# Later layers' constants, weights and first rows loaded and prepared one stage earlier; the second convolution's first group in quarters

## Chip, core and metric

The kernel runs on one core of a Trainium2 chip. The metric is the time of one execution on the device in microseconds (us), as the median of several runs. The core has five engines: TensorE (PE, matmuls, with its weight loads PEld), VectorE (DVE), ScalarE (ACT), GpSimd (POOL) and SyncE (SP), which issues the DMAs.

## What is computed

Four layers on x of 128 graphs, 64 nodes and 256 features, each x = x + f(relu(layernorm(x))). Layer 0 is two graph convolutions and four LSTM passes, layer 1 an attention over 512 edges. Layers 2 and 3 are what the change is about, together with the tables of layer 1:

```python
# layer 2
A_norm = A + jnp.eye(n, dtype=A.dtype)
deg = jnp.sum(A_norm, axis=0) + jnp.sum(A_norm, axis=1) - jnp.diagonal(A_norm)
dinv = jax.lax.rsqrt(deg)
A_hat = A_norm * dinv[:, None] * dinv[None, :]
agg = jnp.einsum('nm,bmd->bnd', A_hat, features)
h = jax.nn.relu(_batchnorm(agg.reshape(-1, d) @ W1.T + b1, g1, be1))
out = _batchnorm(h @ W2.T + b2, g2, be2)
# layer 3
Wh = jnp.einsum('bnf,fo->bno', h, W)
e = (Wh @ a1)[:, :, None] + (Wh @ a2)[:, None, :]
e = jnp.where(e >= 0, e, ALPHA * e)
e = jnp.where(adj_matrix[None] == 0, -jnp.inf, e)
h_prime = jnp.einsum('bij,bjo->bio', jax.nn.softmax(e, axis=-1), Wh)
```

The batch norms of layer 2 need the mean and variance over all 8192 rows, so each of its two products must be finished over all rows before the next stage can begin.

## The kernel before

The 8192 rows are cut into 16 groups (NG) of 512 rows, a group being four tiles of 128 rows (two graphs each). The program is a row of stages, each a block in which every engine runs its own list of instructions; a stage begins on every engine when all engines have ended the stage before. The order inside an engine is the order of the code, and engines wait for each other by semaphores. fp32 products are made as three passes (lines 49 to 51) over a rounded high half and the low rest of each operand.

- `edge_tables` (line 658) sorts the 512 edges and makes the tables of layer 1. It is one long chain on DVE with short turns to PE. Its last steps on DVE are `t_cut` (774), `s_picked` (776), two small copies, `s_weight` (780), which waits for the matmul `s_pW` (809), and eight `t_src`/`t_dst` comparisons (782, 783). SP issues the stage's loads and then the first rows of the next stage. POOL makes low halves of weights there.
- `edge_attention` (813) is layer 1, in four quarters. It ends with additions to rows `c_x` (1426), each stored to `x2` in HBM by SP (920), and SP waits for the last stores to land (line 943).
- `conv_first` (1470) begins with its loads (1511 to 1515): eight small constants, the first two groups of rows `d_xt`, and W1 and W2. DVE adds the identity to the adjacency, PE sums it to degrees, POOL takes deg to the power -0.5 (line 1534, one column), PE spreads that over the columns (1544), and DVE writes `d_hat` (1669). For each group then: statistics on DVE (1616 to 1625), POOL's power -0.5 over four columns (1531), `d_xn` on DVE (1632), relu `d_h` on ACT (1592), aggregation on PE (1561), high half `d_ghi` on ACT (1602), low half `d_glo` on DVE (1681), W1 on PE, the bias on ACT into `H` (1586) and statistics of `H` on DVE (1638). W1 is split before the loop and W2 after it (1643, 1644).
- `conv_second` (1697) loads three small vectors (1719), DVE finishes the first batch norm (1732 to 1737), and for each group ACT makes `f_r` in four instructions (1770), DVE its high and low half (1742, 1744), PE the product with W2, ACT stores it to `H` (1779), DVE takes statistics (1750).
- `dense_attention` (1812) is layer 3. It loads its constants and the first two groups (1879, 1881), finishes the second batch norm (2079 to 2084), folds the vectors a1, a2 into W (2088, 2090), splits W, makes the mask (2098 to 2105), and runs the 16 groups.

## Time and profile before

| | us |
|---|---|
| median of 3 runs | 2231.93 |
| runs | 2231.73 to 2234.61 |
| the profiled execution, its time | 2232.31 |
| its span, first to last instruction | 2230.5 |
| TensorE busy in it | 1993.1 (89%) |
| VectorE busy in it | 1270.4 (57%) |

The profile shows one execution, and its time stands 0.38 us above the median of the runs. A timeline row gives the start in us, the length, the engine, the line and operation, the output and its inputs, and in brackets how long the engine had been idle before and what ended that.

### The profile page before, as it was taken

How to read it: one execution, taken by the hardware profiler on the slowest of the kernel's cores; microseconds unless marked ns; L12 is line 12 of the kernel's file. 1: busy time of each engine (PE TensorE's matmuls, PEld its weight loads, DVE VectorE, ACT ScalarE, POOL GpSimd, SP SyncE). 2: the span in 40 equal slices, each digit the busy share in tenths (PEclk: the TensorE clock that was granted, in tenths of full speed). 3: DMA queues.
4: the chain of work that ended last, by engine and by line, in shares of the span. 5: the costliest groups of instructions: out<-in, count | busy, mean ns of one | idle time of the engine just before them, and what ended most of it. 6: DMA issues, size and time to landing. Idle time of an engine off the chain costs nothing. (4 is left out here: it accounts for less than half of the span.)

```text
span 2230.5 us, 33729 instructions
## 1 busy us (share of the span) xinstructions
PE 1993.1 (89%) x12344; PEld 1633.8 (73%) x12344; DVE 1270.4 (57%) x2673; ACT 981.9 (44%) x1657; POOL 221.3 (10%) x203
## 2 busy tenths in 40 slices
PE   7998999999999999999945998989888688694998
PEld 6997888888999998888833556565655566573887
DVE  7453664454555456445435665656644577674886
ACT  2544663333344333333211653626353245562785
POOL 1000000000111101101102510101000010001100
PEclk9999999999999999999976999999999799896999
DMA  3201010000000000001041223222130311001232
GB/s 109 76 0 38 0 38 1 0 0 38 1 0 0 0 0 0 1 24 52 0 145 48 76 76 107 85 93 90 53 101 11 126 57 38 0 0 59 76 94 86
DMA packets 83582, 100.33 MB, mean 45 GB/s; under 512 B 9248, under 2 KB 75552, under 8 KB 81184
## 3 DMA queue, kind: packets, MB, share of 16 engines
q1 hardware_dynamic: 83488, 99.07, 13.4%
q8 instruction: 60, 0.98, 0.2%
q14 instruction: 34, 0.28, 0.0%
HBM read 62.16 MB, written 33.55 MB: 43 GB/s over the span
## 5 line engine op out<-in xcount | busy, mean ns | idle before, releaser
L535 ACT ACTIVATE b_gate<-b_pG,b_bias 128x512 f32<-128x512 f32 (+1 forms) x504 | 304.4, 633 | 365.8 <-PE b_pG L51 365.2
L49 PE MATMUL b_pG<-b_xshi,b_whi 128*128 128x512 f32 (+1 forms) x1008 | 367.9, 365 | 6.1 <-DVE b_xslo L584 6.0
L50 PE MATMUL b_pG<-b_xslo,b_whi 128*128 128x512 f32 (+1 forms) x1008 | 367.2, 364 | 0.0
L51 PE MATMUL b_pG<-b_xshi,b_wlo 128*128 128x512 f32 (+1 forms) x1008 | 367.1, 364 | 0.0
L580 DVE CAST b_xshi<-HT 128x512 fp32r<-128x512 f32 (+3 forms) x144 | 59.6, 456 | 274.8 <-PE b_pG L51 274.6
L49 PEld LDWEIGHTS b_pG<-b_xshi,b_whi 128*128 128x128 f32 x1008 | 189.9, 188 | 32.7 <-DVE b_xslo L584 6.2
L50 PEld LDWEIGHTS b_pG<-b_xslo,b_whi 128*128 128x128 f32 x1008 | 189.9, 188 | 26.0
L51 PEld LDWEIGHTS b_pG<-b_xshi,b_wlo 128*128 128x128 f32 x1008 | 189.9, 188 | 25.9
L49 PE MATMUL b_pG<-b_hshi,b_whi 128*128 128x512 f32 (+1 forms) x576 | 205.1, 356 | 0.0
L50 PE MATMUL b_pG<-b_hslo,b_whi 128*128 128x512 f32 (+1 forms) x576 | 205.1, 356 | 0.0
L51 PE MATMUL b_pG<-b_hshi,b_wlo 128*128 128x512 f32 (+1 forms) x576 | 205.1, 356 | 0.0
L556 POOL TENSOR_TENSOR b_gate<-b_gate 128x512 f32<-128x512 f32 (+1 forms) x72 | 83.3, 1157 | 931.4 <-ACT b_gate L535 931.4
L543 ACT ACTIVATE b_tc<-b_cell 128x512 f32<-128x512 f32 (+1 forms) x144 | 83.6, 581 | 205.0 <-DVE b_cell L620 105.6
L1221 ACT ACTIVATE c_relu<-c_pZ 128x512 f32<-128x512 f32 x256 | 137.9, 596 | 30.8 <-PE c_pZ L1049 29.9
L50 PEld LDWEIGHTS b_pG<-b_hslo,b_whi 128*128 128x128 f32 x576 | 108.1, 188 | 12.6
L51 PEld LDWEIGHTS b_pG<-b_hshi,b_wlo 128*128 128x128 f32 x576 | 108.1, 188 | 12.4
L49 PEld LDWEIGHTS b_pG<-b_hshi,b_whi 128*128 128x128 f32 x576 | 108.1, 188 | 12.4
L584 DVE TENSOR_TENSOR b_xslo<-HT,b_xshi 128x512 fp32r<-128x512 f32 (+1 forms) x144 | 101.3, 746 | 2.5
L624 DVE TENSOR_TENSOR HT<-b_gate,b_tc 128x512 f32 (+3 forms) x72 | 51.8, 720 | 69.5 <-ACT b_tc L543 69.5
L1049 PE MATMUL c_pZ<-t_both,c_keys 128*128 128x512 f32 x256 | 89.0, 431 | 0.0
L1343 DVE COPY c_vals<-c_pU 128x256 f32<-128x256 f32 x62 | 26.3, 424 | 102.5 <-ACT c_keys L1216 102.2
L627 DVE TENSOR_TENSOR b_tc<-b_gate,b_tc 128x512 f32<-128x512 f32 (+1 forms) x72 | 44.0, 611 | 60.0 <-ACT b_tc L543 60.0
(346 smaller groups left out, 3994.6 us busy)
## 6 DMA issues: line engine op xcount, KB each, us to landing
a_xt<-in_x SPq DMA_DIRECT2D x16, 512.0 KB, 6.0
h_scratch<-HT SPq DMA_DIRECT2D x4, 2048.0 KB, 9.0
c_xt<-in_x SPq DMA_DIRECT2D x16, 512.0 KB, 3.9
c_hst<-h_scratch SPq DMA_DIRECT2D x16, 512.0 KB, 5.0
x_scratch<-c_xt SPq DMA_DIRECT2D x16, 512.0 KB, 2.9
c_x<-x_scratch SPq DMA_DIRECT2D x32, 256.0 KB, 3.9
x_scratch<-c_x SPq DMA_DIRECT2D x32, 256.0 KB, 2.4
d_xt<-x_scratch SPq DMA_DIRECT2D x16, 512.0 KB, 3.7
```

The source lines that it names most:

```text
L49: nc.tensor.matmul(out, w_hi, x_hi, start=first, stop=False)
L50: nc.tensor.matmul(out, w_hi, x_lo, start=False, stop=False)
L51: return nc.tensor.matmul(out, w_lo, x_hi, start=False, stop=last)
L535: nc.scalar.activation(gate[s][:, g, 0:plan.n], pG[s][:, g, 0:plan.n], SIG[g], bias=bias[:, plan.p - 1, 2 * g + s:2 * g + s + 1])\
L543: nc.scalar.activation(tc[s][:, 0:plan.n], cell[b][:, s, 0:plan.n], ACT.Tanh).then_inc(tanh_ready, 1)
L556: nc.gpsimd.tensor_tensor(gate[s][:, I, 0:plan.n], gate[s][:, I, 0:plan.n], gate[s][:, G, 0:plan.n], ALU.mult).then_inc(ig_ready, 1)
L580: nc.vector.tensor_copy(plan.flat(xs_hi[b][:, k, :]), plan.windows(it, b, k, t))\
L584: last = nc.vector.tensor_tensor(plan.flat(xs_lo[b][:, k, :]), plan.windows(it, b, k, t), plan.flat(f32(xs_hi[b][:, k, :])), ALU.subtract)
L624: nc.vector.tensor_tensor(plan.windows(it, b, s, t), plan.flat(gate[s][:, O, :]), plan.flat(tc[s][:, :]), ALU.mult).then_inc(h_ready, 1)
L627: nc.vector.tensor_tensor(tc[s][:, 0:n], gate[s][:, O, 0:n], tc[s][:, 0:n], ALU.mult).then_inc(h_ready, 1)
L1049: nc.tensor.matmul(pZ[i % 2][:, k, :], keys[:, i, k * P:(k + 1) * P], tab["both"][:, :], start=True, stop=True).then_inc(sem["z_mm"], 1)
L1221: nc.scalar.activation(relu_rows[i % RB][:, k, :], pZ[i % 2][:, k, :], ACT.Relu).then_inc(sem["r_done"], 1)
```

## The change

Buffers of the later layers get fixed places in memory (class `Late`), so that they can be filled while an earlier stage runs.

- `edge_tables` now loads the transposed adjacency twice and six small vectors, and computes the degrees and `late.hat` (the normalised adjacency). POOL's power -0.5 is taken there over 64 columns on all partitions, where before it was taken over one column.
- In the last quarter of `edge_attention` SP loads the first two row groups of `conv_first`, W1 and W2. The wait for the last stores moves from the end of `edge_attention` to the start of SP's list in `conv_first`.
- `conv_first` starts with the row statistics; `hat` is two copies; W1 is split between the first and second group; W2 is split at group 14 and no longer after the loop.
- `conv_second` has no load at its start. Its first group goes in quarters of 512 columns through ACT, DVE and PE. It also loads layer 3's constants, and spreads the folding, the splits and the mask over POOL, ACT and DVE beside its loop (DVE: `fold(0)` after group 1, `fold(1)` and `last_weights` at group 14). At its end the first two row groups of layer 3 are loaded.
- `dense_attention` starts with the second batch norm at once.

The diff, cut to its core:

```diff
+                for g in range(TILE_GRAPHS):
+                    sp.dma_start(an_t2[g * NODES:(g + 1) * NODES, :], a["adj_t"]).then_inc(adj_in, 16)
+                for n, t in late.cols.items():
+                    sp.dma_start(t, a[n]).then_inc(late.cols_in, 16)
...
+                pool.wait_ge(deg_ready, 1)
+                nc.gpsimd.tensor_tensor(drow[:, :], deg[:, :], mh[:, :].to_broadcast([P, NODES]), ALU.pow).then_inc(zeroed, 1)
...
+                dve.wait_ge(adj_in, 16 * TILE_GRAPHS)
...
+                link(V.tensor_tensor(eye2[:, :], tab["ident"][:, 0:NODES], tab["ident"][:, NODES:], ALU.add))
+                link(V.tensor_tensor(an_t2[:, :], an_t2[:, :], eye2[:, :], ALU.add))
+                link(V.tensor_tensor(an[:, :], adj[:, :], eye2[r, :], ALU.add))
+                link(V.tensor_tensor(diag[:, :], an[:, :], eye2[r, :], ALU.mult))
+                link(V.tensor_tensor(degs[:, :], an[:, :], an_t2[r, :], ALU.add))
+                V.tensor_tensor(degs[:, :], degs[:, :], diag[:, :], ALU.subtract).then_inc(degs_ready, 1)
                 dve.wait_ge(mm_done, TURNED)
                 V.tensor_tensor(picked[:, :], pD[0:NODES, :], oh_d[0:NODES, :], ALU.mult).then_inc(rows_ready, 1)
...
+                dve.wait_ge(degs_mm, 1)
+                V.tensor_copy(deg[:, :], pH[:, 0:NODES]).then_inc(deg_ready, 1)
                 link(V.tensor_copy(s_col[:, :], pC[:, :, 0]))
                 link(V.tensor_copy(d_col[:, :], pA[:, 0:EDGES:P]))
+                dve.wait_ge(zeroed, 3)
+                link(V.tensor_tensor(pick[:, :], drow[:, :], eye2[:, :], ALU.mult))
+                link(V.tensor_reduce(dcol[:, :], pick[:, :], AX.X, ALU.add))
+                link(V.scalar_tensor_tensor(out=late.hat[:, :], in0=an_t2[:, :], scalar=dcol[:, 0:1], in1=drow[:, :],
+                                            op0=ALU.mult, op1=ALU.mult))
...
+                pe.wait_ge(degs_ready, 1)
+                nc.tensor.matmul(pH[:, 0:NODES], ones[:, :], degs[:, :], start=True, stop=True).then_inc(degs_mm, 1)
...
+                    if last:
+                        sp.wait_ge(sem["t2"], NG)
+                        for b in range(2):
+                            sp.wait_ge(x1_out[b], 16 * NG // 2)
+                            sp.dma_start(late.x[b][:, :, :], x2[b]).then_inc(late.x_in[b], 16)
+                        for t, n in zip(late.w, ("w1", "w2")):
+                            sp.dma_start(t[:, :, :].rearrange("p k c -> p (k c)"),
+                                         late.a[n].rearrange("p k c -> p (k c)")).then_inc(late.w_in, 16)
...
-                    sp.wait_ge(x1_moved[b], 32 * NQ * NH // NR)
+                    late.stored.append((x1_moved[b], 32 * NQ * NH // NR))
...
-                for t, src in loads:
-                    sp.dma_start(t, src).then_inc(sem["consts"], 16)
-                for b in range(2):
-                    sp.dma_start(xt[b][:, :, :], x2[b]).then_inc(landed[b], 16)
-                sp.dma_start(w1[:, :, :], a["w1"]).then_inc(sem["w_in"], 16)
-                sp.dma_start(w2[:, :, :], a["w2"]).then_inc(sem["w_in"], 16)
+                for stored, count in late.stored:
+                    sp.wait_ge(stored, count)
...
-                dve.wait_ge(sem["consts"], 16 * len(loads))
...
-                link(V.tensor_tensor(both[:, :], an[:, :], an_t[:, :], ALU.add))
-                link(V.tensor_tensor(both[:, :], both[:, :], diag[:, :], ALU.subtract))
-                link(V.memset(ones[:, :], 1.0))
-                dve.wait_ge(sem["deg_mm"], 1)
-                link(V.tensor_tensor(pick[:, :], pA[0][:, 0, 0:NODES], eye2[:, :], ALU.mult))
-                V.tensor_reduce(deg[:, :], pick[:, :], AX.X, ALU.add).then_inc(sem["deg_ready"], 1)
...
                 moments(0, 0)
-                normalise(0, 0)
-                moments(1, 1)
-
-                dve.wait_ge(sem["root_ready"], 1)
-                V.tensor_scalar(diag[:, :], eye2[0:NODES, :], dcol[0:NODES, 0:1], None, ALU.mult).then_inc(sem["diag_ready"], 1)
-
-                link(V.tensor_tensor(an_t2[:, :], an_t2[:, :], eye2[:, :], ALU.add))
                 link(V.memset(hat[:, :], 0.0))
-                dve.wait_ge(sem["deg_mm"], 2)
                 for g in range(TILE_GRAPHS):
                     r = slice(g * NODES, (g + 1) * NODES)
-                    last = V.scalar_tensor_tensor(out=hat[r, r], in0=an_t2[r, :], scalar=dcol[r, 0:1], in1=pA[0][r, 1, 0:NODES],
-                                                  op0=ALU.mult, op1=ALU.mult)
-                    last.then_inc(sem["hat_ready"], 1)
+                    V.tensor_copy(hat[r, r], late.hat[r, :]).then_inc(sem["hat_ready"], 1)
+                normalise(0, 0)
+                dve.wait_ge(late.w_in, 32)
+                link(V.tensor_copy(w1_hi[:, :, :], w1[:, :, :]))
+                V.tensor_tensor(w1_lo[:, :, :], w1[:, :, :], f32(w1_hi[:, :, :]), ALU.subtract).then_inc(sem["w1_ready"], 1)
+                moments(1, 1)
                 normalise(1, 1)
-                dve.wait_ge(sem["w_in"], 32)
-                split(w1, w1_hi, w1_lo)
-                V.memset(deg[:, :], 0.0).then_inc(sem["w1_ready"], 1)
...
+                        if isinstance(g, int) and g == NG - 2:
+                            split_w2()
...
-                split(w2, *W2)
...
+                for i in range(2):
+                    wait(pool, sem["folds"], i)
+                    nc.gpsimd.tensor_tensor(late.prod[:, :, :], late.w_raw[:, :, :],
+                                            late.a_row[:, i, :].unsqueeze(1).to_broadcast([P, KD, D]), ALU.mult).then_inc(sem["cleared"], 1)
+                pool.wait_ge(sem["halves"], 1)
+                nc.gpsimd.tensor_tensor(late.w_lo[:, :, :], late.w_raw[:, :, :], f32(late.w_hi[:, :, :]), ALU.subtract)
...
+                def split_first():
+                    for k in range(KH):
+                        if k < KH - 1:
+                            dve.wait_ge(sem["first_relu"], k + 1)
+                            link(V.tensor_copy(r_hi[0][:, k, :], r[0][:, k, :]))
+                            V.tensor_tensor(r_lo[0][:, k, :], r[0][:, k, :], f32(r_hi[0][:, k, :]), ALU.subtract)\
+                                .then_inc(sem["first_lo"], 1)
...
+                        if isinstance(g, int) and g == NG - 2:
+                            fold(1)
+                            last_weights()
                         measure(g, b)
+                        if isinstance(g, int) and g == 1:
+                            fold(0)
...
+                            nc.scalar.activation(late.w_hi[:, :, :], late.w_raw[:, :, :], ACT.Copy).then_inc(sem["halves"], 1)
+                            nc.scalar.activation(late.ident_r[:, :], late.ident[:, :], ACT.Copy)
...
-                fold(0)
                 add_x(0, 0)
                 measure(0, 0)
-                fold(1)
+                V.memset(prob[:, :, :], 0.0)
                 offset(0)
-                weights()
                 lo_halves(0, 0)
                 add_x(1, 1)
                 measure(1, 1)
```

Three places in DVE's list. The first is the end of `edge_tables`; `t_` are its tables, `s_` its working tiles. Before:

```order
L774 TENSOR_SCALAR t_cut<-t_same 128x513
L776 TENSOR_TENSOR s_picked<-s_pD,s_oh_d 64x512
L777 COPY s_s_col<-s_pC 128x4
L778 COPY s_d_col<-s_pA 128x4
L780 TENSOR_SCALAR s_weight<-s_pW 128x512
L782 TENSOR_SCALAR t_src<-s_iota_row,s_s_col 128x64
```

Now (four more 64-column instructions stand ahead of these, after `t_cut`):

```order
L847 TENSOR_TENSOR s_degs<-s_an,s_an_t 64x64
L848 TENSOR_TENSOR s_degs<-s_degs,s_diag 64x64
L850 TENSOR_TENSOR s_picked<-s_pD,s_oh_d 64x512
L852 COPY s_deg<-s_pH 128x64
L853 COPY s_s_col<-s_pC 128x4
L854 COPY s_d_col<-s_pA 128x4
L856 TENSOR_TENSOR s_pick<-s_drow,s_eye 128x64
L857 TENSOR_REDUCE s_dcol<-s_pick 128x1
L858 SCALAR_TENSOR_TENSOR l_hat<-s_an_t,s_dcol,s_drow 128x64
L861 TENSOR_SCALAR s_weight<-s_pW 128x512
L863 TENSOR_SCALAR t_src<-s_iota_row,s_s_col 128x64
```

Between `s_picked` and `s_weight` now stand a copy of the degrees and three instructions that read POOL's result `s_drow`.

The second is the start of `conv_first`; `d_xt` are rows, `d_mv` and `d_rstd` their statistics. Before:

```order
L1653 MEMSET d_ones 64x128
L1655 TENSOR_TENSOR d_pick<-d_pA,d_eye 128x64
L1656 TENSOR_REDUCE d_deg<-d_pick 128x1
L1616 BN_STATS d_st<-d_xt 128x6 x4
L1620 MEMSET d_ve 128x4
L1622 BN_AGGR d_mv<-d_st 128x2 x4
L1625 TENSOR_TENSOR d_ve<-d_ve,d_mv 128x4
L1632 TENSOR_SCALAR d_xn<-d_xt,d_mv,d_rstd 128x256 x4
L1616 BN_STATS d_st<-d_xt 128x6 x4
L1620 MEMSET d_ve 128x4
L1622 BN_AGGR d_mv<-d_st 128x2 x4
L1625 TENSOR_TENSOR d_ve<-d_ve,d_mv 128x4
```

Now, where `l_x` and `l_w` (with a number) are the rows and weights loaded ahead:

```order
L1681 BN_STATS d_st<-l_x_5859 128x6 x4
L1685 MEMSET d_ve 128x4
L1687 BN_AGGR d_mv<-d_st 128x2 x4
L1690 TENSOR_TENSOR d_ve<-d_ve,d_mv 128x4
L1713 MEMSET d_hat 128x128
L1716 COPY d_hat<-l_hat 64x64 x2
L1697 TENSOR_SCALAR d_xn<-l_x_5859,d_mv,d_rstd 128x256 x4
L1719 CAST d_w_hi<-l_w_5861 128x1024
L1720 TENSOR_TENSOR d_w_lo<-l_w_5861,d_w_hi 128x1024
L1681 BN_STATS d_st<-l_x_5860 128x6 x4
L1685 MEMSET d_ve 128x4
L1687 BN_AGGR d_mv<-d_st 128x2 x4
```

The degree work is gone from the head, and W1's split stands ahead of the second group's statistics.

The third is the end of `conv_first` and the start of `conv_second`; `w_hi` and `w_lo` are W2's halves. Before:

```order
L1681 TENSOR_TENSOR d_glo<-d_pA,d_ghi 128x1024
L1638 BN_STATS st<-H 128x6 x8
L1643 CAST w_hi<-d_w 128x1024
L1644 TENSOR_TENSOR w_lo<-d_w,w_hi 128x1024
L1507 UNCONDITIONAL_BRANCH
L1726 UNCONDITIONAL_BRANCH
L1732 BN_AGGR f_mv<-st 128x2 x4
L1733 TENSOR_SCALAR f_ve<-f_mv 128x4
L1735 TENSOR_TENSOR f_scale<-f_g,f_rstd 128x4
L1736 TENSOR_TENSOR f_moved<-f_mv,f_scale 128x4
L1737 TENSOR_TENSOR f_shift<-f_be,f_moved 128x4
L1742 CAST f_rhi<-f_r 128x2048
```

Now the end:

```order
L1728 TENSOR_TENSOR d_glo<-d_pA,d_ghi 128x1024
L1703 BN_STATS st<-H 128x6 x4
L1709 CAST w_hi<-l_w_5862 128x1024
L1710 TENSOR_TENSOR w_lo<-l_w_5862,w_hi 128x1024
L1728 TENSOR_TENSOR d_glo<-d_pA,d_ghi 128x1024
L1703 BN_STATS st<-H 128x6 x8
```

and, further on:

```order
L1811 TENSOR_TENSOR f_moved<-f_mv,f_scale 128x4
L1812 TENSOR_TENSOR f_shift<-l_cols,f_moved 128x4
L1831 CAST f_rhi<-f_r 128x512
L1832 TENSOR_TENSOR f_rlo<-f_r,f_rhi 128x512
L1831 CAST f_rhi<-f_r 128x512
```

W2's split moved ahead of the last `d_glo`, and the first `f_rhi`/`f_rlo` pair of 2048 columns became four of 512.

## Rows read from the trace of the kernel before

**Rows 1.** The page, busy time and share of the span by engine

```profile
PE 1993.1 (89%) x12344; PEld 1633.8 (73%) x12344; DVE 1270.4 (57%) x2673; ACT 981.9 (44%) x1657; POOL 221.3 (10%) x203
```

**Rows 2.** Stretches: length, busy PE, PEld, DVE, ACT, POOL; PEclk; DMA share; GB/s

```profile
1143.00:1190.00 47.00, 9.75 (x22) 5.19 (x23) 22.89 (x54) 3.79 (x6) 4.67 (x8) 0.54 0.48 172
...
1740.00:1760.00 20.00, 1.54 (x5) 1.17 (x6) 8.24 (x39) 1.06 (x1) 2.75 (x4) 0.53 0.45 153
```

**Rows 3.** Timeline of DVE, end of `edge_tables`

```profile
1183.32 0.68 DVE L776 TENSOR_TENSOR s_picked<-s_pD,s_oh_d 64x512 f32<-64x512 f32 x1 [2.69 <-PE s_pD L807]
...
1186.23 0.69 DVE L780 TENSOR_SCALAR s_weight<-s_pW 128x512 f32<-128x512 f32 x1 [1.97 <-PE s_pW L809]
...
1188.86 0.25 DVE L783 TENSOR_SCALAR t_dst<-s_iota_row,s_d_col 128x64 f32<-128x64 f32 x1
```

**Rows 4.** Groups of POOL by form: busy us, mean ns; idle before

```profile
L959 POOL TENSOR_TENSOR c_hst<-c_xt,c_mv 128x512 f32<-128x512 f32 x16 | 16.7, 1042 | 1.3
...
L1724 POOL TENSOR_TENSOR f_rstd<-f_ve,half 128x4 f32<-128x4 f32 x1 | 1.0, 1008 | 26.9 <-DVE f_ve L1733 26.9
L1909 POOL TENSOR_TENSOR e_rstd<-e_ve,half 128x2 f32<-128x2 f32 x1 | 0.7, 698 | 4.1 <-DVE e_ve L2080 4.1
L1534 POOL TENSOR_TENSOR d_dcol<-d_deg,half 128x1 f32<-128x1 f32 x1 | 0.5, 549 | 9.0 <-DVE d_deg L1656 9.0
```

**Rows 5.** Timeline of SP's queue, end of `edge_attention`, start of `conv_first`

```profile
1738.11 2.56 SPq L920 DMA_DIRECT2D x_scratch<-c_x  x2
...
1742.86 0.35 SPq L1511 DMA_DIRECT2D d_eye<-in_ident  x1
```

**Rows 6.** Timeline, start of `conv_first`

```profile
1751.72 1.39 DVE L1616 BATCH_NORM_STATS2 d_st<-d_xt 128x6 f32<-128x256 f32 x4
...
1759.83 6.26 PE L1561 MATMUL d_pA<-d_hat,d_h 128*128 128x128 f32 x32 [0.77 <-DVE d_hat L1669]
...
1761.83 1.22 DVE L1644 TENSOR_TENSOR d_w_lo<-d_w,d_w_hi 128x1024 fp32r<-128x1024 f32 x1
...
1764.70 1.22 DVE L1681 TENSOR_TENSOR d_glo<-d_pA,d_ghi 128x1024 fp32r<-128x1024 f32 x1 [1.53 <-ACT d_ghi L1602]
```

**Rows 7.** Timeline, one turn of `conv_first`'s loop

```profile
1879.87 2.05 PE L1561 MATMUL d_pA<-d_hat,d_h 128*128 128x128 f32 x16 [0.83 <-ACT d_h L1592]
...
1880.77 1.23 DVE L1681 TENSOR_TENSOR d_glo<-d_pA,d_ghi 128x1024 fp32r<-128x1024 f32 x1 [2.04 <-ACT d_ghi L1602]
```

**Rows 8.** Timeline, end of `conv_first`, start of `conv_second`

```profile
1903.49 0.69 DVE L1638 BATCH_NORM_STATS2 st<-H 128x6 f32<-128x512 f32 x1 [0.71 <-ACT H L1586]
...
1909.20 2.46 DVE L1732 BATCH_NORM_AGGREGATE f_mv<-st 128x2 f32<-128x96 f32 x4 [3.17 <-DMA f_b<-in_b]
...
1913.58 5.75 ACT L1770 ACTIVATE f_r<-H,f_shift,f_scale 128x512 f32<-128x512 f32 x8 [10.12 <-DVE f_shift L1737]
...
1920.15 0.80 PE L49 MATMUL f_pO<-f_rhi,w_hi 128*128 128x512 f32 x1 [17.41 <-DVE f_rlo L1744]
```

**Rows 9.** Timeline of DVE, the two splits of 512 columns in `dense_attention`

```profile
2039.84 0.43 DVE L2098 CAST e_w_hi<-e_w_raw 128x512 fp32r<-128x512 f32 x1
2040.30 0.69 DVE L2099 TENSOR_TENSOR e_w_lo<-e_w_raw,e_w_hi 128x512 fp32r<-128x512 f32 x1
```

**Rows 10.** A stretch as in rows 2: PE's first 5.2 us in `conv_second`

```profile
1920.00:1925.20 5.20, 5.05 (x12) 3.99 (x13) 3.52 (x3) 2.93 (x4) 0.00 (x0) 0.50 0.00 0
```

**Rows 11.** Timeline of DVE in `conv_second`'s loop

```profile
1942.07 1.29 DVE L1750 BATCH_NORM_STATS2 st<-H  x2 [2.01 <-ACT H L1779]
...
2015.70 1.29 DVE L1750 BATCH_NORM_STATS2 st<-H 128x6 f32<-128x512 f32 x2 [1.89 <-ACT H L1779]
```

**Rows 12.** Timeline, start of `dense_attention`

```profile
2022.73 0.33 SPq L1879 DMA_DIRECT2D e_ident<-in_ident  x1
...
2027.87 1.21 DVE L2079 BATCH_NORM_AGGREGATE e_mv<-st 128x2 f32<-128x96 f32 x2 [5.39 <-DMA e_adj<-in_adj]
...
2037.86 1.39 POOL L1914 TENSOR_TENSOR e_rstd<-e_ve,half 128x4 f32<-128x4 f32 x1 [7.73 <-DVE e_ve L2126]
```

293 lines of the change are left out of this document (159 added, 134 removed).

## The prediction

> **What bounds the kernel now.** I read the page's busy times first, then the stretches around the starts of the stages, then the timeline of each such start. TensorE is busy 1993.1 us of 2230.5 [rows 1], so the loops inside the stages are near PE's limit, and what PE doesn't do lies mostly where a stage starts. The stretches show it: in the last 47 us of the tables PE has 9.75 us of work, and in 20 us around the start of `conv_first` 1.54 us, at a granted clock of 0.53 [rows 2]. There a chain of small DVE steps, a POOL step and a DMA sets the time. The change shortens three such starts and lengthens a fourth place, the end of `edge_tables`. I add up four moves of a stage's start; a stage that starts earlier ends earlier by as much, unless its loop has another limit, which I look at each time. The sum is made against the profiled execution's 2232.31 us; the median of the runs is 0.38 below it.
>
> **End of `edge_tables`: later.** Six DVE instructions of 64 columns come behind `t_cut`. A comparison of this width takes 0.25 us, with the gap to the next 0.29, so six are 1.7 us, and DVE sat idle 2.69 us there before `s_picked` [rows 3]. They cost nothing; without that cover it would be 1.7. The two adjacency copies and six small vectors that SP issues behind the row loads land long before. PE's extra product has 64 columns and stands ahead of `s_pW`, which waits for `s_picked` anyway: 0 to 0.5, taken as 0. Then the new wait: DVE copies the degrees, POOL takes the power over 64 columns, and DVE waits for it with `s_weight` and the eight comparisons queued behind, then the block's end, on which every engine of `edge_attention` waits. The power's price is the largest unknown. Its rows: one column 0.549 us, two 0.698, four 1.008 [rows 4], a step of 0.15 us a column from one to two and of 0.155 from two to four. Continued to 64, that is 0.55 + 63 x 0.153 = 10.2 us. The other bound is a POOL product of 512 columns in 1.042 us [rows 4], where width costs almost nothing: the power would take about 1.0. I take 10.2, since three rows of the same operation lie on one line and the other row is another operation. The power can start at about 1184.3 (`s_picked` ends at 1184.0, the copy of the degrees 0.2 behind) and ends at 1194.5; the three DVE steps behind it take 0.8 and end at 1195.3. `s_weight` started at 1186.23 [rows 3]. So this stage ends 9.1 us later; with a power of 1.0 it is 0, since those 2.2 us are DVE's wait for PE.
>
> A rule speaks against that line. The Trainium skill, GPSIMD Engine Reference, section 3.1 (Elementwise, side-by-side cycle accounting), gives about 2.6 cycles at 1.2 GHz for each element of an operation with two inputs. By it, an estimate, 63 more columns cost 0.14 us and the power about 0.7 us. The product of 512 columns agrees with that rule, the three power rows do not, and they decide; what the rule gives for the time is the first rival.
>
> **The last quarter of `edge_attention`: nothing.** SP gets four more transfers behind its four fetches, once the last rows are turned (about 1656). The next thing SP has to do is a store about 68 us later, so neither the queue nor the 2 MB meet anything. Without that cover it would be SP's four issues, about 2 us.
>
> **Start of `conv_first`: earlier.** SP's last issue ends at 1740.67, and the next stage began at 1742.86, as SP waited for the stores to land [rows 5]. That wait now stands in the next stage, where only SP's reload behind it needs it. The step from one stage to the next costs 0.25 to 0.5 us: `conv_second`'s DVE ends at 2027.87 - 5.39 = 2022.48 and SP starts at 2022.73 [rows 12]. So DVE can take the first row statistics at about 1741.1 and no longer at 1751.72 [rows 6]: 10.6 us. Does it reach PE and the loop? From the first statistics to the first `d_glo` it was 1764.70 - 1751.72 = 12.98 us [rows 6]. In the new order DVE does statistics, the two `hat` copies under POOL's power, `d_xn`, W1's split (0.68 and 1.22), statistics of group 1, POOL's power, `d_xn`; ACT then its relu and `d_ghi`: by the rows' lengths 13.05 us, the same. PE's first product starts at 1746.8 for 1759.83, its second group waits for ACT until about 1753, and W1's product starts near 1757 for 1766.1, partly at the lower clock, so PE at first gains only 8 us. But the loop isn't PE's: a turn takes 9.05 us, in which PE waits 0.83 us for the relu and DVE 2.04 us for ACT [rows 7], and the circle DVE-ACT sets it. PE catches up 1 us a turn, over 14 turns. I take 10.6; the bounds are 8 (PE never catches up) and 11.
>
> **From `conv_first` to `conv_second`: earlier.** The last statistics of `H` end at 1903.49 + 0.69 = 1904.18 and the batch norm starts at 1909.20, after W2's split and 3.17 us of waiting for three loads [rows 8]. With both gone it starts at about 1904.55: 4.65 us. W2's split, 1.93 us, moves ahead of `d_glo` of group 15. PE works on group 14 then and has 2.4 us before it needs that half, so it costs 0; without this cover it would be 1.9.
>
> **The first group in quarters: earlier.** From ACT's first relu to PE's first product it was 1920.15 - 1913.58 = 6.57 us [rows 8]: four relus, then both halves of 2048 columns. A quarter takes ACT 5.75 / 8 = 0.72 to 0.8 us [rows 8] and DVE 0.43 + 0.69 [rows 9] and 0.05 between them, so PE starts 2.05 us after the first relu: 4.5 us earlier. Then DVE feeds a quarter each 1.17 us. PE's three passes on it take 3 x 0.43 = 1.3 us at the granted clock of 0.50 it has there, 1.2 GHz (12 matmuls in 5.2 us [rows 10]), so PE doesn't run dry, and its clock rises as early after its start as before. DVE's splits cost 4 x 1.17 = 4.7 us for 3.5, but are ready for group 1 before PE is. I take 4.5, bounds 2 and 4.5.
>
> **In the loop of `conv_second`.** `fold(0)` adds 0.69 us of DVE behind the statistics of group 1. The odd groups' splits are ready just as PE needs them, so it shifts these, and 0.5 us of it reaches the end (0 to 0.7). `fold(1)`, two small casts and two halves of the mask at group 14 add 1.65 us, where DVE idled 1.89 [rows 11]. ACT's two copies and POOL's work lie in their idle time. The new row loads end before they are needed.
>
> **Start of `dense_attention`: earlier.** DVE waited 5.39 us for the loads and began at 2027.87 [rows 12]; now it begins 0.35 after 2022.48: 5.0 us. POOL's power beside DVE's folding took 1.39 us [rows 12] where others take 1.01 [rows 4]; the folding is gone, so 0.3 more. The rest of the removed weight work lay under ACT's and PE's steps. Bounds 4.7 and 5.6.
>
> **The sum.** + 9.1 - 10.6 - 4.65 - 4.5 + 0.5 - 5.3 = -15.4 us. 2232.31 - 15.4 = 2216.9 for the profiled execution, 2216.5 for the median.
>
> **Rivals.** (1) The power over 64 columns is cheap, about 1 us, as POOL's other wide products are. Then the tables cost 0 and the sum is -24.5: 2207.4. For it: the product of 512 columns; against it: three rows on a line, all of them narrow. Chance 0.14. (2) The gains are partly given back inside the loops: in `conv_first` PE stays the bound and only 8 us arrive, in `conv_second` PE runs dry between quarters, its clock stays low through the first group and 2.5 us of the 4.5 go. Together 5.1 less: 2221.6. For it: PE's wait in `conv_first` is only 0.83 us a turn, and the quarters have a margin of 0.1 us each; chance 0.15. (3) Slower: the power is worse than its line, say because it now reads its exponent from a repeated column and runs through 64 columns on all partitions. The tables would have to lose more than 24.5 us for a loss, a power of over 26 us, that is 0.39 us a column, 2.6 times the rows. At three times the rows' price the power is 30.6 us and the time 2237. Against it: nothing in the rows grows faster than the line; the worst seen was 1.39 for 1.01. Chance 0.03. (4) The change doesn't do what it says: each stage's start has another late comer (the moved loads, a semaphore of the tables), and what is gained there is no more than the power costs: 2229 to 2232. Nothing in the rows names one. Chance 0.04.
>
> **How the numbers follow.** The forecast, 2213 to 2221, has 0.64. The range takes in rival 1 down to 2206 and rival 2 up to 2223, and leaves out some 0.15. About 0.2% (4.5 us) is what a measurement of this kernel can tell from no change. Forecast, rivals 1 and 2 are all faster by more than that: 0.93. Same: rival 4, 0.04. Slower: 0.03.
>
> **What would show it.** In the new profile POOL has one power of 128x64; 10.2 us proves the line, 1 us the first rival. DVE's idle time before the instruction behind it should be 10 us. `s_weight` to the stage's end stays 2.9 us. The first statistics of `conv_first` should follow SP's last issue by 0.5 us and `d_glo` 13 us later; the turns of the loop should stay at 9.05. The batch norm should start 0.4 us after the last statistics of `H`, PE's first product 2 us after the first relu with no gaps in the first twelve passes, and `dense_attention` should begin with its batch norm 0.4 us after the last statistics. The forecast is wrong if the power's price is off the line, or if a start moves and its stage's end doesn't.

## The result, and the profile after

The changed kernel takes 2219.53 us (median; 2217.02 to 2222.29), the kernel before beside it 2233.27 (2231.73 to 2235.73). The ratio of the changed kernel's time to that of the kernel before is 0.9935, with a 95% interval of 0.9922 to 0.9948: 14.5 us (12 to 17) less, of 2233. The forecast was 2216.5 us, with 2206 to 2223 as its range.

The profiled execution of the changed kernel took 2217.02 us with a span of 2215.2, 15.3 less than the 2230.5 before. Its busy times are those of [rows 1] within 6 us, but for POOL, which has 17 us more:

```profile
PE 1991.8 (90%) x12342; PEld 1628.6 (74%) x12342; DVE 1269.8 (57%) x2672; ACT 981.9 (44%) x1659; POOL 238.1 (11%) x208
```

So the work stayed and the waits went. I laid the two traces side by side from one marker to the next; a marker is the start of an instruction that both kernels have. `e_off` and `e_hTlo` are tiles that DVE writes in the dense stage, `e_off` first for group 0 and `e_hTlo` once a group. All are in us, and the last column is what the prediction had there.

| from | to | before | after | difference | predicted |
|---|---|---|---|---|---|
| 0 | last `t_cut` | 1180.20 | 1179.40 | -0.80 | 0 |
| last `t_cut` | last `t_dst` | 8.66 | 18.12 | +9.46 | +9.1 |
| last `t_dst` | last addition into `c_x` | 550.72 | 551.69 | +0.97 | 0 |
| last addition | first row statistics of `conv_first` | 12.14 | 1.54 | -10.60 | -10.6 |
| first statistics | last statistics of `H` | 151.77 | 151.68 | -0.09 | 0 |
| last statistics | `f_mv` | 5.71 | 1.01 | -4.70 | -4.65 |
| `f_mv` | group 0 is kept | 19.17 | 16.31 | -2.86 | -4.5 |
| group 0 kept | group 15 kept | 91.43 | 93.21 | +1.78 | +0.5 |
| group 15 kept | `e_mv` of the batch norm | 8.07 | 2.98 | -5.09 | -5.0 |
| `e_mv` | first `e_off` | 11.49 | 10.89 | -0.60 | -0.3 |
| first `e_off` | third `e_hTlo` | 39.55 | 36.78 | -2.77 | 0 |
| third `e_hTlo` | end | 151.59 | 151.59 | 0 | 0 |

"Kept" is ACT's `f_unused` instruction, which waits for the group's last product. The rows of the changed kernel that answer to those of before follow, from timelines (start, duration, engine, line, operation, idle time before it and what ended it).

The end of the tables, answering to [rows 3]. POOL's power stands alone for 10.52 us, DVE waits as long, and what is behind it takes 3.5 us:

```profile
1182.45 0.68 DVE L850 TENSOR_TENSOR s_picked<-s_pD,s_oh_d 64x512 f32<-64x512 f32 x1 [1.10 <-PE s_pD L888]
1183.44 10.52 POOL L787 TENSOR_TENSOR s_drow<-s_deg,s_mh 128x64 f32<-128x64 f32 x1 [7.37 <-DVE s_deg L852]
1194.06 0.23 DVE L856 TENSOR_TENSOR s_pick<-s_drow,s_eye 128x64 f32<-128x64 f32 x1 [10.51 <-POOL s_drow L787]
1194.90 0.69 DVE L861 TENSOR_SCALAR s_weight<-s_pW 128x512 f32<-128x512 f32 x1
1197.52 0.25 DVE L864 TENSOR_SCALAR t_dst<-s_iota_row,s_d_col 128x64 f32<-128x64 f32 x1
```

The start of `conv_first`, answering to [rows 5] and [rows 6]. The first statistics come 1.5 us behind the last addition, while the stores are still on their way (the DMA engines are 90% busy from 1750.75 to 1751.50):

```profile
1749.21 0.69 DVE L1517 TENSOR_TENSOR c_x<-c_pU,c_x 128x512 f32<-128x512 f32 x1 [2.08 <-DMA c_x<-x_scratch]
1750.75 1.41 DVE L1681 BATCH_NORM_STATS2 d_st<-l_x 128x6 f32<-128x256 f32 x4 [0.84 <-PEq L969]
1756.56 3.72 PE L1626 MATMUL d_pA<-d_hat,d_h 128*128 128x128 f32 x16 [8.47 <-ACT d_h L1657]
1763.59 1.22 DVE L1728 TENSOR_TENSOR d_glo<-d_pA,d_ghi 128x1024 fp32r<-128x1024 f32 x1 [2.03 <-ACT d_ghi L1667]
```

The start of `conv_second` with its quarters, answering to [rows 8] and [rows 10]. Beside POOL's clearing the first cast `f_rhi` of 512 columns takes 0.71 us, where it takes 0.42 alone; beside POOL's product the second `f_rlo` quarter takes 1.65 us where the others take 0.69, and PE runs dry for 0.63 us:

```profile
1903.44 2.46 DVE L1807 BATCH_NORM_AGGREGATE f_mv<-st 128x2 f32<-128x96 f32 x4 [0.31 <-PEq L1582]
1907.81 5.75 ACT L1879 ACTIVATE f_r<-H,f_shift,f_scale 128x512 f32<-128x512 f32 x8 [5.41 <-DVE f_shift L1812]
1908.57 0.52 POOL L1788 MEMSET l_other<- 128x512 f32 x1
1908.66 0.71 DVE L1831 CAST f_rhi<-f_r 128x512 fp32r<-128x512 f32 x1 [0.88 <-ACT f_r L1879]
1909.40 0.69 DVE L1832 TENSOR_TENSOR f_rlo<-f_r,f_rhi 128x512 fp32r<-128x512 f32 x1
1910.15 0.80 PE L52 MATMUL f_pO<-f_rhi,w_hi 128*128 128x512 f32 x1 [8.47 <-DVE f_rlo L1832]
1910.48 1.34 POOL L1796 TENSOR_TENSOR l_prod<-l_w_raw,l_a_row 128x512 f32<-128x512 f32 x1
1910.72 1.65 DVE L1832 TENSOR_TENSOR f_rlo<-f_r,f_rhi 128x512 fp32r<-128x512 f32 x1
1912.43 0.79 PE L52 MATMUL f_pO<-f_rhi,w_hi 128*128 128x512 f32 x1 [0.63 <-DVE f_rlo L1832]
```

TensorE's clock stays at its lower level for 7.0 us behind PE's first product, for 5.2 before the change. As in [rows 10] (length, busy PE, PEld, DVE, ACT, POOL; PEclk; DMA share; GB/s):

```profile
1910.10:1917.10 7.00, 6.32 (x14) 4.50 (x15) 6.86 (x8) 6.02 (x9) 1.64 (x2) 0.50 0.00 1
```

Three groups later POOL's two last operations meet the split of a whole group. They take 2.2 and 3.4 us, where 1.3 was enough for the first of these products, and `f_rlo` of 2048 columns 3.27 instead of 2.29:

```profile
1928.59 1.22 DVE L1817 CAST f_rhi<-f_r 128x2048 fp32r<-128x2048 f32 x1
1928.75 2.21 POOL L1796 TENSOR_TENSOR l_prod<-l_w_raw,l_a_row 128x512 f32<-128x512 f32 x1 [16.93 <-DVE l_wa L1843]
1929.84 3.27 DVE L1819 TENSOR_TENSOR f_rlo<-f_r,f_rhi 128x2048 fp32r<-128x2048 f32 x1
1930.92 3.35 POOL L1799 TENSOR_TENSOR l_w_lo<-l_w_raw,l_w_hi 128x512 fp32r<-128x512 f32 x1
```

The four don't share, they take turns. DVE's cast ends at 1929.81 and POOL's product 1.15 us later, at 1930.96. DVE's subtraction ends 2.15 us behind that, at 1933.11, about its own length of 2.29, and POOL's next operation at 1934.27, 1.16 us later, where 1.3 is its length alone. So each ran when the other had ended. The Trainium skill (SBUF — State Buffer, section "SBUF: two separate sides") has a rule for this: VectorE and GpSimd share one pair of memory ports, and when VectorE's operation is of a kind that needs that pair (a fast mode with two ports, or two inputs from SBUF beside a GpSimd operation that reads SBUF), whichever of the two starts first has the pair for the whole instruction and the other stands. The trace agrees with the turns, by the figures above; which kinds of operation need the pair no run here shows.

The start of `dense_attention`, answering to [rows 12]: 1.6 us from the last statistics to its first operation.

```profile
2014.35 1.29 DVE L1825 BATCH_NORM_STATS2 st<-H 128x6 f32<-128x512 f32 x2 [4.53 <-ACT H L1890]
2015.94 1.21 DVE L2166 BATCH_NORM_AGGREGATE e_mv<-st 128x2 f32<-128x96 f32 x2 [0.30 <-PEq L1774]
```

So the sum, -15.3 against a predicted -15.4, is right partly by luck: the quarters gave 1.6 us less than forecast, the loop behind them 1.3 less, the attention stage 1.0 less and the tables 0.4 less, while the dense stage gave 3.2 more and the part ahead of the tables 0.8. The experiments ask what the table can't answer: the power's price, what the quarters are worth by themselves, what the loop of `conv_second` lost, which of the early loads carry the gain, and whether the 0.97 and the 2.77 us belong to the change at all.

### The profile page after: what moved, and what is told of

It reads as the page before. It is cut to its first block and busy times, and to the rows that moved or that the text cites. A ratio compares the mean times of both kernels' runs of the same rounds, so it can differ in the third digit from the quotient of the medians.

```text
span 2215.2 us, 33755 instructions
## 1 busy us (share of the span) xinstructions
PE 1991.8 (90%) x12342; PEld 1628.6 (74%) x12342; DVE 1269.8 (57%) x2672; ACT 981.9 (44%) x1659; POOL 238.1 (11%) x208
```

## The experiments

All but one start from the changed kernel. Markers as in the table; whole times are medians, beside the kernel before on the same chip.

**The changed kernel again.**

> The changed kernel as it is, on the same chip as the next three: 2217 to 2222 us, a ratio to the kernel before of 0.9922 to 0.9948. It also tells which differences between the two traces belong to the change and which to one execution. If the earlier rise of TensorE's clock in the dense stage (windows 2040:2050 at 0.66, 2050:2060 at 1.00, against 0.53 and 0.83 at the same place of the kernel before) belongs to the change, it is there again, and the dense loop is again 2.8 us shorter; if it was this execution's, the part from the first e_xn to the end changes by 1 us or more. The last 1.0 us of the attention stage, where stores and fetches wait for one another, should also show which it is.

2217.52 us, ratio 0.9925 (0.9904 to 0.9945). Every stretch of the table agrees with the first profile within 0.25 us but two: the part ahead of the last `t_cut` took 1178.16 us, 1.2 less, and the attention stage 554.51 instead of 551.69. TensorE's clock was low there twice more. The same stretches of the two executions, this one first (length, busy PE, PEld, DVE, ACT, POOL; PEclk; DMA share; GB/s):

```profile
1514.00:1520.00 6.00, 5.93 (x14) 3.25 (x14) 0.00 (x0) 1.17 (x3) 0.00 (x0) 0.51 0.62 206
1594.00:1598.00 4.00, 3.20 (x8) 2.58 (x9) 0.66 (x1) 0.00 (x0) 0.00 (x0) 0.62 0.00 0
```

and the first profile of the changed kernel:

```profile
1514.00:1520.00 6.00, 5.06 (x18) 2.56 (x22) 0.79 (x1) 1.34 (x3) 0.00 (x0) 0.72 0.70 217
1594.00:1598.00 4.00, 3.63 (x16) 2.97 (x17) 1.61 (x5) 0.00 (x0) 0.00 (x0) 1.00 0.00 0
```

The granted clock is at 0.50, 1.2 GHz, for one more short time, and stays there longer another time. So nothing is read from that stage's length in one execution if it is under about 4 us.

**The power over one column.**

```
-  tensor_tensor(drow, deg, mh.to_broadcast([P, NODES]), ALU.pow)
+  DVE:  pick = pH * eye2;  deg[:, 0:1] = sum of pick
+  POOL: dcol = deg[:, 0:1] pow mh                       one column
+  DVE:  diag = eye2 * dcol                              ahead of s_weight
+  PE:   pH[:, 64:128] = ones x diag                     behind s_pW
+  DVE:  late.hat = (an_t2 * dcol) * pH[:, 64:128]       behind the last t_dst
```

> The power in the edge tables is taken over one column (the degrees are picked out first, and the row of the roots is made by a second product of ones with a diagonal tile, as the kernel before did it), and the normalised adjacency is the last operation of the tables. Theory, the power is paid by the column: POOL's instruction falls from 10.52 us to about 0.55, nothing waits for it (the product with the picked weights is later), and the tables end 8.5 to 9.5 us earlier: 2209 to 2211 us, ratio to the kernel before 0.989 to 0.991. Rival, the tables' length is set by the other new operations (copies, sums and products on VectorE, 3 to 4 us in all): then only 6 us or less come back, 2213 to 2216.

2207.46 us, ratio 0.9883 (0.9864 to 0.9902), 10.1 us under the changed kernel beside it. From the last `t_cut` to the last `t_dst` it takes 8.52 us, for 18.13 with the wide power and 8.66 before the change. Nothing of the new work but the last 0.28 us is on the path:

```profile
1184.34 0.55 POOL L787 TENSOR_TENSOR s_dcol<-s_deg,s_mh 128x1 f32<-128x1 f32 x1 [7.63 <-DVE s_deg L853]
1185.95 0.69 DVE L859 TENSOR_SCALAR s_weight<-s_pW 128x512 f32<-128x512 f32 x1 [0.70 <-PE s_pW L893]
```

DVE waits for PE here, as it did before the change, and not for POOL. The theory holds and the rival falls. The edit also took three short DVE steps (0.84 us in all) from behind the power, so at least 8.8 of the 9.6 us are the power's width; the last experiment, which puts 5.4 us of power back into the new order and gets 4.96 us, says that nearly all is.

**What a power costs by its shape.**

```
+  for rows, w, op in ((128, 8, pow), (128, 16, pow), (128, 32, pow), (128, 128, pow),
+                      (64, 64, pow), (128, 64, mult), (128, 512, mult)):
+      gpsimd.tensor_tensor(tro[0:rows, 0:w], tri[0:rows, 0:w], mh.to_broadcast([rows, w]), op)
```

> Seven operations on a scratch tile are added on POOL in the edge tables, where it waits anyway, each finished before the next: the power with 128 partitions over 8, 16, 32 and 128 columns, the power with 64 partitions over 64 columns, and a product with 128 partitions over 64 and 512 columns. Theory, a power costs 0.155 us a column beside 0.4 (0.55, 0.70 and 1.01 us at 1, 2 and 4 columns, 10.5 at 64): 1.6, 2.9, 5.4 and 20.2 us. Rival 1, the 128x64 power was dear for another reason (a broadcast operand, the wait ahead): then 32 and 128 columns do not lie on the line. If the price is by the column alone, the 64 partitions cost 10.3 us too; if it is by the element, about 5.3. The product over 64 columns should cost below 0.6 us. The time of the whole tells nothing.

POOL's groups by form (busy us, mean ns; idle before):

```profile
L791 POOL TENSOR_TENSOR s_tro<-s_tri,s_mh 128x128 f32<-128x128 f32 x1 | 20.7, 20726 | 0.1
L795 POOL TENSOR_TENSOR s_drow<-s_deg,s_mh 128x64 f32<-128x64 f32 x1 | 10.5, 10517 | 0.1
L791 POOL TENSOR_TENSOR s_tro<-s_tri,s_mh 64x64 f32<-64x64 f32 x1 | 10.5, 10508 | 0.1
L791 POOL TENSOR_TENSOR s_tro<-s_tri,s_mh 128x32 f32<-128x32 f32 x1 | 5.4, 5413 | 0.1
L791 POOL TENSOR_TENSOR s_tro<-s_tri,s_mh 128x16 f32<-128x16 f32 x1 | 2.9, 2901 | 0.1
L791 POOL TENSOR_TENSOR s_tro<-s_tri,s_mh 128x8 f32<-128x8 f32 x1 | 1.8, 1807 | 0.1
...
L791 POOL TENSOR_TENSOR s_tro<-s_tri,s_mh 128x512 f32<-128x512 f32 x1 | 1.0, 1038 | 0.1
...
L791 POOL TENSOR_TENSOR s_tro<-s_tri,s_mh 128x64 f32<-128x64 f32 x1 | 0.3, 292 | 0.1
```

From 32 to 128 columns a column costs (20726 - 5413) / 96 = 160 ns, from 8 to 16 it is 137. With [rows 4] the step is 150 ns up to 4 columns and 200 ns from 4 to 8. It is nearly a line with a step of about 0.16 us, and half the partitions cost the same. A product of the same 64 columns costs 0.29 us, a 36th, and each further column of it (1038 - 292) / 448 = 1.7 ns.

**The first group whole again.**

```
-  split_first()
+  split(0, 0)                       and PE waits for lo_done of group 0 as of any other
```

> The first group of the second convolution goes whole again, as before; everything else stays. Theory, the quarters gave 4.2 us at the first product, 2.9 of which were still there when group 0 was kept: the first product comes 4.2 us later, and the time is 2.5 to 3.5 us longer than the changed kernel's, 2221 to 2223. Rival 1, what the quarters gave was lost through work of POOL beside VectorE's splits, and without quarters this loss stays: then the time is 4.2 us longer, 2224. Rival 2, the loop makes up for a late start (its turn has slack, so that a later first group is caught up): less than 1 us longer, 2220.

2225.01 us, ratio 0.9955 (0.9939 to 0.9972), 7.5 us over the changed kernel beside it; no theory had so much. By the stretches, PE's first product comes 7.24 us behind the first relu instead of 2.34, so the quarters are worth 4.9 us there; at the end of group 0 it is 2.57 (19.10 us from `f_mv` for 16.53), which is what the theory had (2.5 to 3.5) and not the 4.2 of rival 1. The loop is as long as with quarters, 93.23 us, so rival 2 falls. A further 2.4 us are in the dense stage, 39.30 us from `e_off` to the third `e_hTlo` for 36.92: TensorE's clock was low there twice and not once. Between the two profiled executions, 7.1 us apart, the rest is 1.95 us ahead of the last `t_cut` and 0.6 at the dense stage's end, less 0.4 in the attention stage: stretches that the edit doesn't touch. The first group whole shows the neighbour too: its cast takes 1.90 us for 1.23 before the change, beside POOL's first product.

```profile
1913.44 1.27 POOL L1796 TENSOR_TENSOR l_prod<-l_w_raw,l_a_row 128x512 f32<-128x512 f32 x1
1913.89 1.90 DVE L1817 CAST f_rhi<-f_r 128x2048 fp32r<-128x2048 f32 x1 [3.00 <-ACT f_r L1879]
1915.83 2.29 DVE L1819 TENSOR_TENSOR f_rlo<-f_r,f_rhi 128x2048 fp32r<-128x2048 f32 x1
```

**POOL's work in the second convolution put off.**

```
+  for i, t in enumerate((wa_hi, wa_lo, mask, own)):
+      pool.wait_ge(sem["o_done"], 3 + i);  gpsimd.memset(t, 0.0)
   for i in range(2):
-      wait(pool, sem["folds"], i)
+      pool.wait_ge(sem["o_done"], 8 + i)
       gpsimd.tensor_tensor(prods[i], w_raw, a_row[i], mult)     second one into the memory of `other`
+  other, w_lo: behind fold(1);  ACT's w_hi: with group 14;  fold(0): with group 14, ahead of fold(1)
```

> POOL's clearing and folding of the last layer's weights, and ScalarE's rounding of them, leave the first groups of the second convolution: the clearing is spread over groups 3 to 6, the two products over groups 8 and 9, the rest is in the last two groups. Theory, these operations slow VectorE's splits when they run beside them (512 columns 0.69 to 1.65 us, 2048 columns 2.29 to 3.27) and cost 1.4 us in the quarters and 1 us in groups 2 and 3: 1.5 to 2.5 us less than the changed kernel, 2217 to 2218; quarter 1's f_rlo takes 0.7 us again. Rival, the slow splits come from the tiles' place or from TensorE's clock, not from POOL: f_rlo of quarter 1 still takes over 1.2 us and nothing comes back. Second rival, the work costs the same wherever it runs in this loop, as every split is on the path: the start is shorter, the loop longer, the time within 0.7 us of the changed kernel's.

2215.79 us, ratio 0.9918 (0.9901 to 0.9935). From `f_mv` to the first kept group it takes 14.47 us for 16.53, and from there to the last one 92.09 for 93.21: 2.06 and 1.12 us. Every quarter takes its 0.69 us now, and group 0's products follow one another:

```profile
1909.92 0.69 DVE L1838 TENSOR_TENSOR f_rlo<-f_r,f_rhi 128x512 fp32r<-128x512 f32 x1
1910.98 0.69 DVE L1838 TENSOR_TENSOR f_rlo<-f_r,f_rhi 128x512 fp32r<-128x512 f32 x1
1912.05 0.69 DVE L1838 TENSOR_TENSOR f_rlo<-f_r,f_rhi 128x512 fp32r<-128x512 f32 x1
...
1918.71 0.20 ACT L1893 ACTIVATE f_unused<-f_scale 128x1 f32<-128x1 f32 x1 [1.53 <-PE f_pO L54]
```

So the quarters without their neighbour give 19.17 - 14.47 = 4.70 us, the 4.5 of the prediction; the neighbour took 2. PE's first product comes 2.06 us behind the first relu, 4.51 earlier than the 6.57 before the change. (The stretch to the first kept group spreads with the moment at which TensorE's clock rises: 18.8 and 19.2 us in the two profiles of the kernel before, 15.5 to 16.8 in eight with quarters and the neighbour, 14.1 to 14.5 in three without it. They don't overlap.) Both rivals fall, the second because the loop got shorter too: where POOL's operations stand now they lengthen no split, and POOL's products take 1.30 us each. The whole time, 1.7 us under the changed kernel, is within the spread.

**The second convolution's tiles 32 bytes further.**

```
-  unused = sb("f_unused", [P, 1])
+  unused, _ = sb("f_unused", [P, 1]), sb("f_pad", [P, 1])
```

> A column of 32 bytes is put ahead of the second convolution's tiles, so that its input tiles (f_r, f_rhi, f_rlo) lie at the same offset from a multiple of 64 bytes as in the kernel before; nothing else changes. In the loop of the second convolution a product of 512 columns starts every 0.2285 us in the kernel before and every 0.2335 in the changed one, which makes some 1 to 1.8 us over the sixteen groups. Theory, this comes from where the tiles lie: the spacing is 0.2285 again and the stretch from the first kept group to the last 0.7 to 1.8 us shorter (93.21 us with the tiles as they are). Rival, it comes from something else (the first group's other rhythm, the slower copies): the stretch stays at 93.2 within 0.2 us. The whole time tells little here, 2216 to 2221.

2219.33 us (2215.42 to 2223.55), which says nothing. From the first kept group to the last it is 92.20 us for 93.21, 1.0 less. In stretches of 8 to 10 us between 1950 and 1970 the products of this tile show it (duration in ns, lowest, median, highest). Before the change, the changed kernel, and the changed one moved by 32 bytes:

```profile
L50 PE MATMUL f_pO<-f_rlo,w_hi x12: 392/392/394, 1950.0 to 1957.6; 128*128 128x512 f32 x12
```

```profile
L53 PE MATMUL f_pO<-f_rlo,w_hi x13: 392/396/396, 1960.2 to 1968.8; 128*128 128x512 f32 x13
```

```profile
L53 PE MATMUL f_pO<-f_rlo,w_hi x13: 387/389/390, 1960.2 to 1969.7; 128*128 128x512 f32 x13
```

On average over 8 us a product starts 0.229 us behind the other before the change, 0.233 in the changed kernel, 0.230 with the shift. The tiles' place does it: the change gave up three small tiles ahead of them, and by the programs' addresses their start moved from 32 to 0 bytes behind a multiple of 64. By what mechanism is open: in `conv_first` the input tiles moved as well, from 0 to 32, and a product starts every 0.233 us in both kernels.

**The first rows and weights loaded late again.**

```
   edge_attention, SP, last quarter:   - dma_start(late.x[b], x2[b]) twice; - dma_start(w1), dma_start(w2)
   conv_first, SP, behind the waits for late.stored:   + the same four
```

> The first two row tiles and both weights of the first convolution are loaded at its own start again, behind the wait for the last stores; the constants and the normalised adjacency stay prepared ahead. Theory, of the 10.6 us between the last addition of the attention stage and the first statistics most is the loads: the wait for the last stores (about 2 us) and then the rows' landing (2 to 3 us) come in series ahead of the first statistics, so that 5 to 6 us come back, and the weights' landing hides behind the first group: 5 to 6 us more than the changed kernel's, 2223 to 2225, and the stretch from the last addition to the first statistics is 1.5 us with early loads and 6.5 to 7.5 without. Rival, the stage's start was set by the constants and the chain that made the adjacency, and the rows landed beside it: then the loads cost 3 us or less, 2220 to 2222.

2227.56 us, ratio 0.9965 (0.9952 to 0.9978). From the last addition to the first statistics 6.82 us for 1.54: 5.28 us, as the theory has it. The loads stand behind the stores, and DVE waits for them:

```profile
1756.66 0.93 SPq L1580 DMA_DIRECT2D l_x<-x_scratch  x2
...
1760.53 1.41 DVE L1678 BATCH_NORM_STATS2 d_st<-l_x 128x6 f32<-128x256 f32 x4 [6.12 <-DMA l_x<-x_scratch]
```

The weights' landing did not hide wholly: DVE's split of W1 waits 0.31 us for it, and the stage takes 0.4 us longer. The rows' 5.28 us are half of the 10.6 us; the other half, 12.14 - 6.82 = 5.3, is what preparing the adjacency and the constants ahead gave. The whole is 7 to 9 us longer, more than the 5.7 of the stretches up to `f_mv`; 2.6 of the rest are again the dense stage's clock (39.54 us from `e_off` to the third `e_hTlo`). The attention stage took 555.26 us, so the four early transfers are not what lengthens it. That the other half is the constants and the adjacency is the remainder, not a test of its own; for it, before the change DVE waited for the constants until 1749.00 and began its statistics 2.72 us behind that, behind the adjacency's steps.

**The split of the second weights behind the last statistics again.**

```
   conv_first, DVE:   - split_w2() in the turn of group 14;   + split_w2() behind measure(15)
```

> The split of the second convolution's weights goes back behind the last statistics of the first one; the loads of its constants stay early. Before, 5.71 us lay between the last statistics' start and the second convolution's first operation. Theory, the split (0.68 and 1.23 us) and the wait for the constants (3.17 us of idle, part of it what a new stage costs anyway) each had a share: with the split after, 1.9 to 2.0 us of the 4.7 come back, the rest stays gone. The whole is 2.0 us above the changed kernel's, 2219 to 2222. Rival, the two lay beside one another (the constants were on their way while VectorE split, so that taking away one alone gives nothing): then less than 0.5 us comes back.

2223.30 us, ratio 0.9930 (0.9907 to 0.9954). From the last statistics to `f_mv` 3.09 us for 1.01: 2.08 come back, as expected. The other 2.6 of the 4.7 are the remainder; before the change DVE waited there for the constants' loads [rows 8], and now only 0.31 us passes there, the step between two stages. The whole is again more than that, with the dense stage at 39.51 and the attention stage at 555.01 us.

**The dense stage's first rows loaded at its own start again.**

```
   conv_second, SP:       - wait for relu_done 16, dma_start(again[b], x2[b]) twice
   dense_attention, SP:   + the two loads ahead of steps()
```

> The first two row tiles of the dense stage are loaded at its own start again; its constants, weights and mask stay prepared ahead. Theory, the 5.1 us at this stage's start came from the constants and the weights' preparation alone: the rows are first used 6.5 us after the stage's first operation and land in 2 to 3 us, so that nothing changes, within 0.2 us in the stretch from the stage's first VectorE operation to the first turned rows, and the time is that of the changed kernel within its noise, 2216 to 2221. Rival, the rows are late: 1 us or more in that stretch. By the first theory the early loads of the rows are not worth their waits in the second convolution; a third reading, that these loads cost something there (they run beside the last two groups), shows as a stretch from group 0's keeping to the dense stage's first operation that is shorter than 96.2 us.

2220.03 us, ratio 0.9916 (0.9893 to 0.9938). From `e_mv` to the first `e_off` 10.89 us with or without; from group 0 kept to `e_mv` 96.23 for 96.18. These two loads moved without any effect: so the stage's 5.1 us are the constants, for which DVE waited 5.39 us before the change [rows 12].

**Three repairs together.** The one-column power, POOL's work put off, and the 32 bytes.

> The changed kernel with three things together: the power over one column and the adjacency's last operation at the end of the tables; POOL's clearing and folding spread over the later groups of the second convolution; the second convolution's tiles moved by 32 bytes. Theory, they lie in different places and add up: 9.6 us in the tables, 2.1 at the first kept group, 1.1 in the loop by POOL and 1.0 by the tiles' place, 13.8 in all from 2219.5: 2205.7 us, a ratio to the kernel before of 0.9865 to 0.9885; the stretch from the first kept group to the last is 91.1 us (93.21 in the changed kernel, 91.43 in the kernel before). Rival, POOL's work and the tiles' place are one cause seen twice, and give 1.1 together in the loop: the stretch is then 92.1 and the time 2206.8. Second rival, TensorE's clock takes some of it back by a further fall in the attention or the dense stage, 1.5 to 3.5 us each: the single stretches are as above, the whole 2207 to 2209.

2201.67 us (2200.12 to 2206.74), the kernel before beside it 2238.04, ratio 0.9849 (0.9829 to 0.9870). Last `t_cut` to last `t_dst` 8.52 us; `f_mv` to the first kept group 14.15. From the first kept group to the last it is 91.17 us, for 92.09 with POOL's work put off alone and 93.21 in the changed kernel. So the 1.12 and the 0.92 add up, and POOL's work and the tiles' place are two causes. By the stretches 9.6 + 2.16 + 2.04 = 13.8 us are gone from the changed kernel, as expected, but the whole is 4 us under the 2205.7 expected: the ratios say 17 to 19 (0.9849 against 0.9925 and 0.9935), which the intervals allow to be 14. The second rival's further fall of the clock did not come. The attention stage took 550.62 us, 1.1 to 3.9 less than in the two profiles of the changed kernel.

**The kernel before again, and a longer table.** Up to here the attention stage had taken 550.6 to 550.7 us in three executions with short tables and 551.7 to 555.3 in nine with long ones (the run with the powers of several sizes, whose tables were the longest, took 552.79). That looked like a cost of the long table beyond its own 9.6 us.

```
+  gpsimd.tensor_tensor(drow[:, 0:32], deg[:, 0:1].to_broadcast([P, 32]), mh.to_broadcast([P, 32]), pow)
```

is the second kernel's edit, ahead of the one-column power of the three repairs.

> The kernel before, profiled once more. The attention stage (from the last entry of the tables to the last addition) takes 550.6 to 550.7 us in the three kernels whose tables end at 1187 to 1189 us, and 551.7 to 555.3 in the eight whose tables end at 1196 to 1199; TensorE's clock falls up to two times more there. Theory, the longer tables bring this about, and the kernel before shows 550.7 again, with the same four falls after 1370 us. Rival, it is chance: the stage shows anything between 550.6 and 555. In the dense stage its clock should show which of two courses it takes: with a second fall some 45 us after the first one (as in its first profile) or without.

> The best kernel so far, with a power over 32 columns (5.4 us) whose result nobody uses ahead of the power over one column in the edge tables. The tables become 5.4 us longer less what lies beside them (0.8 to 1.5 us): 12.4 to 13.4 us instead of 8.52 from the last cut to the last entry. Theory 1, TensorE's clock and with it the attention stage go by how long TensorE stood idle in the tables: the attention stage takes 553 to 555 us instead of 550.6, and the whole is 7 to 9 us longer than the best kernel's, 2209 to 2211 (ratio to the kernel before 0.988 to 0.990). Theory 2, it goes by where the pieces of work fall in time, which no rule made here foretells: the stage takes anything from 550.6 to 555. Rival, the attention stage has nothing to do with the tables' length: 550.6 plus chance, and the whole 4 to 5 us longer, ratio 0.987.

The kernel before took 2236.39 us and this time 554.72 us in the attention stage. The same stretch in its two executions, the first profile and this one:

```profile
1588.00:1591.00 3.00, 3.00 (x14) 2.27 (x13) 2.79 (x8) 0.00 (x0) 0.00 (x0) 1.00 0.00 0
```

```profile
1588.00:1591.00 3.00, 3.00 (x8) 2.35 (x8) 0.08 (x1) 0.00 (x0) 0.00 (x0) 0.50 0.00 0
```

In all, TensorE's clock is at 1.2 GHz for 6.6 us more of this stage in the second execution. So the longer stage comes without any change of the kernel, and the theory falls. The longer table says so too: 13.48 us from the last `t_cut` to the last `t_dst` (12.4 to 13.4 expected), 4.96 more, an attention stage of 549.98, and a profiled span of 2203.5 for 2199.9. Its median, 2207.46 (2205.13 to 2215.62), with a ratio of 0.9890 (0.9861 to 0.9919), is too wide to tell the rival from the theories. In the dense stage the kernel before took 39.22 us from `e_off` to the third `e_hTlo`, with a second time of low clock as in its first profile.

## Why the prediction was right, and where it was not

**The tables, +9.1: right, +9.46.** The line through one, two and four columns, 10.2 us, met 10.52, and these 0.3 us are nearly all of the miss. Rivals 1 and 3 hang on the same number and fall with it. The Trainium skill's rule (GPSIMD Engine Reference, section 3.1), 2.6 cycles at 1.2 GHz for an element of an operation with two inputs, comes near the products here: 448 more columns cost 0.75 us, 0.97 by the rule, an estimate. It misses the power: 63 more columns cost 10.52 - 0.55 = 9.97 us.

**Nothing in the last quarter of the attention stage: right in substance.** The 0.97 us of the first profile are within what this stage differs by itself, 550.72 and 554.72 for the kernel before.

**`conv_first`'s start, -10.6: right**, and for the reasons given. The loop did not give it back: 5.8 us from the first statistics to PE's first product (5.7 predicted), 12.84 to the first `d_glo` (13.05 predicted), and turns of 9.05 us as in [rows 7]:

```profile
1878.81 2.05 PE L1626 MATMUL d_pA<-d_hat,d_h 128*128 128x128 f32 x16 [0.82 <-ACT d_h L1657]
1879.70 1.22 DVE L1728 TENSOR_TENSOR d_glo<-d_pA,d_ghi 128x1024 fp32r<-128x1024 f32 x1 [2.04 <-ACT d_ghi L1667]
```

In seven of the twelve executions with the change TensorE's granted clock fell once more, to 0.50, some 13 us into the stage, in the others not. From the first statistics to the last ones of `H` it took 151.7 to 151.8 us in eleven of them, with or without that fall, whether the clock was low for 7 us there or for 18, and 152.1 in the twelfth, the one with the loads late, where DVE waited for W1: PE isn't the bound there, and its clock doesn't matter. Half of the 10.6 is the loads; the other half, by what remains, the constants and the adjacency.

**`conv_second`'s start, -4.65: right, -4.70**; 2.1 of it is W2's split and 2.6, by what remains, the loads.

**The quarters, -4.5: wrong by 1.6 in this kernel.** The step that failed is that DVE feeds a quarter each 1.17 us to PE's 1.3, "so PE doesn't run dry, and its clock rises as early after its start as before". The durations were taken from a place where POOL was idle [rows 9], and in this same change POOL gets its clearing and its product behind its power, beside exactly these splits. With POOL quiet the term is 4.70, and 4.3 to 5.0 over the profiles at hand. The loss has three parts. The first product came 4.23 us earlier and not 4.5, for the slower first cast. PE then ran dry for 0.63 us. The last 0.75 us go with the clock, which rose 7.0 us behind the first product and not 5.2; at the low clock a product starts every 0.43 us, at the high one every 0.23. In the eight profiles with quarters and the neighbour PE runs dry for 0.62 to 0.63 us each time, and the clock rises 5.3 to 8.1 us behind the first product (4.1 to 4.8 in the three without the neighbour). In the two where it rises at 5.3 the stretch from the first product to the kept group is 8.8 us for 8.2 before the change: there the dry time alone is lost. That the dry time delays the clock's rise fits this but was not tested apart. Rival 2 named PE running dry between the quarters and its clock staying low, and that is what happened, about two thirds of its 2.5 us, but it gave no cause. Rival 4 falls: none of the four starts had another late comer.

**The loop, +0.5: mis-sized, +1.78.** "ACT's two copies and POOL's work lie in their idle time" was true for ACT and POOL, and false for DVE, on whose splits POOL's work ran. Putting it off, and `fold(0)` with it, gave 1.12 us; how much of that is `fold(0)`, for which I had 0.5, was not told apart. The tiles' place, of which I had nothing, gave 0.9 to 1.0. With both undone the loop is 2.04 us shorter than in the changed kernel, 0.3 shorter than before the change.

**`dense_attention`, -5.3: -5.09 and -0.60: right to 0.4.** The constants carry it, the rows nothing, as their first use is 6.5 us later.

**The 2.77 us in the dense loop: not predicted, and not settled.** Where the clock falls a second time within the first 50 us of the stage, `e_off` to the third `e_hTlo` takes 38.9 to 39.6 us (both executions of the kernel before and four of the changed ones), else 36.8 to 37.3 (eight of the changed ones). So a kernel with the change can go either way. Whether the change makes the better course likelier, or whether that is chance in two executions of before, stays open.

## What to carry to other kernels

Price an operation moved onto a parallel engine by its own rows at its own width, and before making it wider to save a step elsewhere, see whether the narrow form hides: here a power over one column and one more small product cost nothing, and over 64 columns, with three short steps behind it, 9.6 us. When work is put onto POOL beside a critical copy of DVE, the copy stands while it runs, so put it where DVE waits. Compare two kernels stretch by stretch between markers, profile the kernel before a second time, and don't explain a difference that it shows against itself.

## What the runs showed of the hardware

- A power on POOL costs some 0.16 us a column (0.14 to 0.20 from one width to the next) and the same on 64 or 128 partitions: 0.55, 0.70 and 1.01 us for 1, 2 and 4 columns [rows 4], 1.81, 2.90, 5.41, 10.52 and 20.73 us for 8, 16, 32, 64 and 128. A product of 64 columns takes 0.29.
- POOL and DVE hold one another up, one operation at a time. A split of 512 columns took 1.65 us for 0.69 and one of 2048 columns 3.27 for 2.29; POOL's operations of 512 columns took up to 2.21 and 3.35 us for 1.3. The 2048-column cast took 1.90 us for 1.23 beside POOL's product, and the 512-column cast 0.71 for 0.42 beside its clearing.
- The same products of 512 columns start every 0.229 or 0.233 us by where the stage's tiles lie in memory; a shift by 32 bytes changes it in `conv_second`. It was worth 1.0 us in 16 groups. In `conv_first` a like shift changed nothing.
- From one stage's last DVE operation to the next one's first it is 0.3 us at the two convolutions' ends, 0.85 at the attention stage's.
- With unchanged code the attention stage took 550.7 and 554.7 us, with one more time and one longer time of TensorE's clock at 1.2 GHz, 6.6 us more of it in all.
